# Twelve identity products on the tensor engine ahead of the moments of tiles 1 to 3 of a recommendation tower

## What is computed

```python
def _cin_layer(x_prev, x0, W, b):
    return jnp.einsum('bik,bjk,hij->bhk', x_prev, x0, W) + b[None, :, None]

e = jnp.stack([tbl_0[ids[:, 0]], ..., tbl_25[ids[:, 25]]], axis=1)   # 512 x 26 x 32
x1 = _cin_layer(e, e, W1, b1)
x2 = _cin_layer(x1, e, W2, b2)
z = jnp.sum(jnp.concatenate([x1, x2], axis=1), axis=-1)              # 512 x 256
h = jnp.concatenate([z, dense_ctx], axis=1)
h = jnp.maximum(h @ W_top1 + b_top1, 0.0)                            # 272 -> 512
h = jnp.maximum(h @ W_top2 + b_top2, 0.0)                            # 512 -> 256
y = h @ W_top3                                                       # 256 -> 1
```

## Time and profile before

| what | value |
|---|---|
| median of 3 runs | 290.71 us |
| lowest and highest run | 289.09, 292.08 us |
| the profiled execution, its own time | 289.82 us |
| its span, first to last instruction | 288.1 us |
| PE busy | 161.0 us, 56% of the span |
| POOL, DVE, ACT busy | 100.1, 97.5, 56.7 us |
| granted PE clock, mean | 0.738 of full speed |

### The profile page before, as it was taken

One profiled execution on the slowest core, in us unless ns is written; L12 is line 12 of the kernel. 1 busy time (PEld: TensorE's weight loads), 2 busy tenths in 40 slices (PEclk: granted clock), 3 DMA queues, 4 the chain that ended last, 5 costly groups with the idle time before them and its releaser, 6 DMA issues.

```text
span 288.1 us, 3079 instructions
## 1 busy us (share of the span) xinstructions
PE 161.0 (56%) x1193; PEld 146.8 (51%) x1193; DVE 97.5 (34%) x341; ACT 56.7 (20%) x156; POOL 100.1 (35%) x110
## 2 busy tenths in 40 slices
PE   8764221121111111111114449799999999999996
PEld 8753221011010101011014339799999999999995
DVE  2400000000000302100019996499249826973100
ACT  1021000000000000000032423602450245026312
POOL 5777777777777777774000000000000000000000
PEclk9995555555555555555555769979999999999999
DMA  6910110001101101100000000000000000000000
GB/s 228 354 17 12 14 15 14 12 14 14 14 12 14 14 11 15 14 13 9 0 0 0 0 0 3 1 2 0 2 0 2 0 2 1 2 0 2 2 0 0
DMA packets 5217, 5.97 MB, mean 21 GB/s; under 512 B 2226, under 2 KB 4402, under 8 KB 5203
## 3 DMA queue, kind: packets, MB, share of 16 engines
q0 software_dynamic: 3328, 1.71, 4.2%
q1 hardware_dynamic: 1410, 2.52, 2.7%
q10 hardware_dynamic: 464, 1.54, 1.5%
HBM read 5.77 MB, written 0.00 MB: 20 GB/s over the span
## 4 chain that ended last, share of the span: by engine, by line
PE 42%; another core or an unknown queue 35%; DVE 8%; issue 8%; ACT 3%; DMA 3%; SPq 0%
PE bank L252 12%; PE bank L253 6%; PE bank L259 5%; PE bank L263 4%; DVE folded L497 4%; PE bank L219 3%; DMA w2t<-in_w2t_dram 3%; PE bank L266 3%; PE bank L298 3%; PE bank L285 2%; PE bank L283 2%; ACT folded L345 1%; DVE diag L459 1%; PE bank L288 1%
## 5 line engine op out<-in xcount | busy, mean ns | idle before, releaser
L199 POOL DMA_INDIRECT rows<-in_tbl_dram,idx x104 | 99.4, 956 | 32.9 <-issue 31.4
L224 PE MATMUL bank<-w1s,w2t 128*128 128x169 f32 x52 | 21.9, 473 | 100.4 <-issue 97.1
L224 PEld LDWEIGHTS bank<-w1s,w2t 128*128 128x128 f32 x52 | 14.5, 301 | 107.4 <-issue 103.6
L252 PE MATMUL bank<-diag,prod 128*128 128x108 f32 x256 | 49.3, 293 | 1.4 <-DVE prod L623 1.4
L497 DVE TENSOR_TENSOR folded<-folded 128x6 f32<-128x6 f32 (+15 forms) x44 | 5.6, 177 | 108.6 <-issue 99.5
L252 PEld LDWEIGHTS bank<-diag,prod 128*128 128x128 f32 x256 | 38.8, 192 | 1.8 <-ACT v L351 1.8
L253 PE MATMUL bank<-diag,prod 128*77 128x64 f32 x256 | 36.9, 226 | 0.0
L253 PEld LDWEIGHTS bank<-diag,prod 128*77 128x77 f32 x256 | 30.9, 148 | 0.0
L486 DVE COPY t<-bank 13x128 f32<-13x128 f32 (+1 forms) x64 | 16.8, 263 | 31.7 <-PE bank L253 31.0
L345 ACT COPY folded<-bank 128x366 f32<-128x366 f32 x13 | 6.0, 465 | 84.1 <-remote 65.4
L373 ACT COPY t<-bank 55x256 f32<-55x256 f32 (+2 forms) x48 | 14.1, 294 | 28.2 <-PE bank L253 27.9
(11 more groups left out here) (55 smaller groups left out, 168.3 us busy)
## 6 DMA issues: line engine op xcount, KB each, us to landing
rows<-in_tbl_dram,idx POOLq DMA_INDIRECT x104
wt<-in_W_top_dram SPq DMA_DIRECT2D x2, 512.0 KB
w2t<-in_w2t_dram ACTq DMA_DIRECT2D x1, 832.0 KB
w2t<-in_w2t_dram SPq DMA_DIRECT2D x1, 832.0 KB
w1t<-in_w1t_dram ACTq DMA_DIRECT2D x1, 640.0 KB
w1p<-in_w1p_dram SPq DMA_DIRECT2D x1, 521.0 KB
idx<-in_ids_dram SPq DMA_DIRECT2D x1, 39.0 KB
dctx<-in_dctx_dram ACTq DMA_DIRECT2D x1, 32.0 KB
```

The source lines that it names most:

```text
L199: pool.indirect_dma_start(rows[t][:, f, :], None, tables[f], bass.IndirectOffsetOnAxis(ap=idx[:, t, f:f + 1], axis=0)).then_inc(s_got[t][p ...
L224: mm = nc.tensor.matmul(ps[:, i * CROSS:(i + 1) * CROSS], w2t[:, lo + x0 + i, :], w1s[:, c0:c0 + CROSS], start=True, stop=True)
L252: nc.tensor.matmul(m0[:, a0:a0 + JW * QUADS], prod[:, G, 0:P], mov, start=True, stop=True)
```

## The change

A helper `keep_clock(t)` is called at the start of `moments(t)` for tiles 1, 2 and 3. It waits until the transposes of part 1 of tile `t` are done, and then multiplies the identity by itself twelve times into the first 128 columns of bank 2. Nothing reads these results; the moments overwrite them. The wait for the products of the first half, `s_pa`, stands behind them as before.

```diff
@@ -74,6 +74,7 @@
 WARM = 24
+FILL = 12
 D_CTX = 16
@@ -233,7 +234,15 @@
+            def keep_clock(t):
+
+                pe.wait_ge(s_turn[1], t + 1)
+                for _ in range(FILL):
+                    nc.tensor.matmul(bank[2][:, 0:P], ident[:], ident[:], start=True, stop=True)
+
             def moments(t):
+                if t:
+                    keep_clock(t)
                 pe.wait_ge(s_pa, t + 1)
                 for s in range(STEPS):
```

## The result

The changed kernel takes 297.96 us (median of 4 runs, 296.43 to 299.06) against 289.9 us before (4 runs, 288.33 to 292.08). The ratio is 1.0269, with a 95% interval of 1.0177 to 1.0361: 2.7% slower. Throughout, a ratio is taken over undisturbed executions alone, those within 1.5% of the same kernel's fastest, while a median is over all, so that one low execution of before can move a ratio by about 1% where the medians are equal.

A forecast was written before the change was run, and what follows sets the result against it. PE was taken to bound tiles 1 to 3, with no idle time for the products. 72 records at 0.112 us add 8.1 us, the wait 0, to the median of 290.71: 298.8 us, range 296.7 to 301.2.

The forecast's parts named there:

- What bounds the kernel: PE bounds tiles 1 to 3, busy at clock 1.00; the gap ahead of the moments is 0.01 us.
- The price: 72 matmul records ahead of the moments of tiles 1 to 3, 0.112 us each: 8.1 us, bounds 8.0 and 8.7.
- The wait: Wait on the transpose ahead of tiles 1 to 3's moments: met long before; seams 0 to 0.6 us in all, taken as 0.
- The total: Median 290.71 + 8.1 = 298.8 us, 2.8% more; for the profiled execution 289.82 + 8.1 = 297.9 us.
- B: Products keep PE's clock at tiles 1 to 3, saving at most 5.0 us for 8.1 spent: 293.8 us; chance 0.03.
- C: Longer program shifts the setup's 38 waits at L224, 2.6 us each; four gone give 288.6 us; chance 0.02.
- D: Products run off PE's path or their repeated weight loads are skipped: half price, 4.0 us, 294.7 us; chance 0.04.
- E: Products run at or leave the clock at 1.2 GHz: 72 x 0.213 = 15.3 us, 306.0 us; chance 0.02.
- F: No change: products hidden by a wait that modelled matmul ends conceal, 290.7 us; chance 0.02.

The follow-up runs named there:

- late fields: Eight unused DVE fills ahead of the first half's products of tiles 1 to 3, against before (290.23 us): 321.21 us; with the change's twelve products too, 317.09 us.
- the clock kept for tile 0: Without the change's products: thirty ahead of the setup's last transposes, six behind them, against before (287.87 us): 286.28 us, ratio 0.9999.
- the run with sixteen products: Without the change's products: sixteen ahead of the setup's last transposes, eight in tile 0's 1.8 us wait, against before (290.23 us): 290.43 us, ratio 1.0148.

## Why the prediction was right, and where only in part

**What bounds the kernel.** Right for the chip the prediction was about. PE was on the path at the seam, the three groups of products stood on the chain for their full length, and nothing gave the time back. Two readings were loose, and no number hung on them: PE waits 1.4 us for DVE at the start of tile 0's moments as well, and the clock's line stands at 9 in the first three slices and at 7 and 6 in slices 23 and 24, where the text has 0.5.

**The price.** 72 x 0.112 = 8.1 us was predicted. The profile gave 3 x 2.68 = 8.0, that is 0.112 a record, as L207 had shown. The estimate from the Trainium skill ("TensorE: Matmul & The Clock Gate", section "Back-to-back issue gap"), 5.8 us, was not borne out. One moving column did not change that pace, so the load is enough to set it.

**The wait.** At zero, as taken.

**The total.** 298.8 predicted and 297.96 measured, 8.06 us above the median of before as it came out (289.9 instead of 290.71). The profiled execution was 299.06 instead of 297.9, for the 1.2 us ahead of the first product; the prediction took the setup and tile 0 as unchanged, and in the profiles of the slow chips the moments of tile 0 begin anywhere from 165.74 to 173.77. The difference was predicted for a reason; that the absolute time fell into a range of 4.5 us built on three runs of before had luck in it: the same change later had a median of 294.54, below the range, beside a before of 287.87.

**The rivals.** B stays a matter of place: it needs a fall ahead of tiles 1 to 3, and none was there; with late fields it came true. Its reading that the clock fell behind the 1.8 us wait of tile 0 does not hold in every execution: the profile after has the same wait and 1.00 behind it. C rested on a supply of instructions that sets the 97.1 us at L224, and the ten products in the setup cost nothing there, so the count of instructions does not set it. In the profile after, the waits for "issue" at this line came to 95.7 us and those at L220 to 6.9, against 97.1 and 4.4 (L219): moved a little, 1.1 us more in all. D and E are out by L241's 2.68 us at clock 1.00. F, hidden, is out here by the period of 29.92 us.

**What the prediction could not see.** It called the fields landed "long before" from one profile. That holds because the slow setup there lets the gathers finish (last issue 132.76) before the tiles begin. Where the setup is quick, the gathers end last and the same twelve products cost nothing that the measurement can tell. The argument was right and its premise belonged to the slow setup.

**Open.** Why PE is through the groups of L224 at 128 to 154 us in some groups of runs and at 30 in others was not settled, nor whether that goes with the chip. The slow stretch affects PE, DVE and ACT at once and ends about 16 us behind the last gather's issue, but no run took the gathers away. Whether the clock kept for tile 0 gains time is open too, being smaller than the spread.

## What to carry to other kernels

Before filling an engine's time with warm-up work, find the wait that it is to fill, in the chain, ahead of that place: without one, the filler costs its full length, count times pace. Then see how the filler lies in the wait: one that ended 0.89 us before the real work kept the whole clock, those that ended 1.59 and 2.68 us before it kept part, one that ended 4.49 us before the transposes left the moments of tile 0 at 0.50, and one that began at a fallen clock lasted up to twice as long. Do not make it narrow: one moving column cost the same and did not keep the clock. And a gap can be there on one chip and not on another: look at a second one before building on it.

## What the runs showed of the hardware

- The same kernel took about 290 us on some chips and 185 on others. On the first, one load or matmul of PE stood every 1.40 us in the setup until about 149 us (or until its groups were done). On the second they did not (the 52 of L224 took 7.62 us in all, from 21.97), while gathers took longer (the last at 144.95 instead of 132.76).
- The clock at PE: after waits of 6.58 to 7.49 us ahead of the moments it stood at 0.50 for their first 4 to 5 us. In the run with sixteen products it was 1.00, and 0.50 again behind 4.49 us of idleness, a short burst of transposes and another 2.09 us. With the thirty and six it stayed at 1.00 across waits of 1.10 and 1.51 us.
- With no wait of PE at all, the clock fell to 0.52 from 83.4 to 86.9 behind 24 records of one moving column (2.74 us); behind 24 of 128 columns it stayed at 1.00 in the profile after. The former is one execution.
- Behind the same 1.8 us wait of PE in tile 0 the clock was 0.63 in the profile before and L259 took 4.80 us (as in late fields), and 1.00 and 3.17 us in the profile after.
- A float32 product with a 128-column weight takes as long with one moving column as with 128: 2.74 and 2.84 us for 24 records, each with the last record's modelled length.
